# The weights stage of a graph kernel: one scalar_tensor_tensor for each tile in place of two operations for eight tiles

## What is computed

```python
def _L0_gnn_ref(x, edge_index, W, att, bias):
    h = (x @ W).reshape(N, H, C)
    row, col = (edge_index[0], edge_index[1])
    alpha = leaky_relu(s_src[row] + s_dst[col], negative_slope=0.2)
    ...
    alpha_n = ex / denom[row]
    msg = alpha_n[:, :, None] * h[col]
    out = jax.ops.segment_sum(msg, col, num_segments=N)
    return out.reshape(N, H * C) + bias
```

## Time and profile before

| | |
|---|---|
| median of three runs | 6992.02 us |
| span of the profiled execution, first to last instruction | 5519.0 us |
| difference of the two | 1473.02 us |
| PE busy (share of the span) | 4135.2 us (75%) |
| DVE busy | 3665.8 us (66%) |
| ACT busy | 3051.7 us (55%) |
| POOL busy | 3822.1 us (69%) |
| mean granted clock of PE | 0.901 |

### The profile page before, as it was taken

The page is one execution under the profiler, slowest core; times in us unless marked ns, Lnnn a source line. Parts: engine busy times, 40 slices in busy tenths (PEclk is TensorE's granted clock), DMA queues, the critical chain, the costliest instruction groups (busy, mean ns, idle before and its releaser), DMA issues. The chain is left out here.

```text
span 5519.0 us, 98800 instructions
## 1 busy us (share of the span) xinstructions
PE 4135.2 (75%) x22700; PEld 3433.9 (62%) x22897; DVE 3665.8 (66%) x7986; ACT 3051.7 (55%) x4595; POOL 3822.1 (69%) x3494
## 2 busy tenths in 40 slices
PE   4777777777777777600799977887888877887877
PEld 4666666666666666500799965666666666666665
DVE  7865444444444444439999997777777777777774
ACT  4455555545454555401677746666666666666663
POOL 2347777777777777740599955777777777777773
PEclk9988888888888888755899989999999999999998
DMA  8765555555555555494100035555555555555557
GB/s 306 262 199 148 141 139 141 139 139 139 141 139 142 138 142 140 144 68 12 57 0 0 0 78 139 145 147 146 146 144 146 146 146 146 144 146 147 146 141 104
DMA packets 1199545, 722.20 MB, mean 131 GB/s; under 512 B 929434, under 2 KB 1018452, under 8 KB 1199388
## 3 DMA queue, kind: packets, MB, share of 16 engines
q1 hardware_dynamic: 843788, 332.57, 29.7%
q0 software_dynamic: 131616, 276.04, 17.4%
q10 hardware_dynamic: 224112, 113.25, 7.2%
HBM read 559.64 MB, written 161.88 MB: 131 GB/s over the span
## 5 line engine op out<-in xcount | busy, mean ns | idle before, releaser
L1030 POOL DMA_INDIRECT g_q<-q_d,g_aux x1664 | 1574.5, 946 | 640.1 <-issue 472.4
L562 POOL DMA_INDIRECT rec_d<-rec,place x1568 | 1528.2, 975 | 499.0 <-issue 475.9
L1328 PE MATMUL g_hp<-pw,g_mix 128*128 x3328 | 883.3, 388 | 270.9 <-ACT g_mix L1224 253.4
L673 PE MATMUL lk<-tab_sd,low 128*128 128x196 f32 x3136 | 1063.1, 427 | 0.0
L1339 PE MATMUL g_ap<-g_hid,g_oh 128*128 128x256 f32 x3328 | 898.7, 393 | 165.7 <-DVE agg L1122 149.9
L611 DVE TENSOR_REDUCE rank<-equal 128x4 f32<-128x512 bf16 x392 | 262.0, 684 | 1019.1 <-ACT equal L539 1008.5
L1244 ACT ACTIVATE g_hid<-g_q 128x512 f32<-128x512 f32 x832 | 524.0, 630 | 744.8 <-DVE g_q L1108 716.2
L1108 DVE TENSOR_TENSOR g_q<-g_hp,g_q 128x512 f32<-128x512 f32 x832 | 574.8, 691 | 506.0 <-DMA g_q<-q_d,g_aux 440.6
L1328 PEld LDWEIGHTS g_hp<-pw,g_mix 128*128 128x128 f32 x3328 | 620.5, 191 | 430.3 <-issue 353.1
L1339 PEld LDWEIGHTS g_ap<-g_hid,g_oh 128*128 128x128 f32 x3328 | 587.0, 191 | 364.7 <-issue 275.1
L670 PE MATMUL lk<-mask,hx 122*128 122x245 bf16 x1568 | 483.8, 309 | 429.7 <-ACT low L528 429.7
(11 more groups left out here) (233 smaller groups left out, 5557.7 us busy)
## 6 DMA issues: line engine op xcount, KB each, us to landing
low_row<-rows_d SPq DMA_DIRECT2D x392, 256.0 KB
g_ea<-rec_d SPq DMA_DIRECT2D x208, 256.0 KB, 4.2
rec<-in_ea ACTq DMA_DIRECT2D x196, 256.0 KB
rec_d<-pad ACTq DMA_DIRECT2D x49, 936.0 KB, 3.8
hx_row<-rows_d SPq DMA_DIRECT2D x392, 98.0 KB
g_lrow<-low_row_d SPq DMA_DIRECT2D x208, 128.0 KB
g_q<-q_d,g_aux POOLq DMA_INDIRECT x1664, 2.8
rec_d<-rec,place POOLq DMA_INDIRECT x1568
```

Of the source, the lines that this page charges most:

```text
L562: pool.indirect_dma_start(rec_d, bass.IndirectOffsetOnAxis(ap=place[0:n, at, j:j + 1], axis=0), rec[0:n, at, j, :], None).then_inc(s_sc[at ...
L673: mm = pe.matmul(to[:, NB:LK], low[:, par, 1, slots], tab_sd[:, :, :].rearrange("p h a -> p (h a)"), start=False, stop=True, skip_group_ch ...
L1030: pool.indirect_dma_start(qg[:, par, j, :], None, q_d, bass.IndirectOffsetOnAxis(ap=aux[:, par, j, F_IDX - F_LOW:REC - F_LOW].bitcast(I32) ...
L1328: mm = pe.matmul(hp[u][:, k * HID:(k + 1) * HID], mix[:, par, 2 * u + k, :], pw[:, bass.ds(b[k], 1), :].rearrange("p o f -> p (o f)"), sta ...
```

## The change

For each of the eight tiles of a group, one scalar_tensor_tensor compares 0 to 48, read again for each of the four heads, with the tile's column of `high_dst`, and multiplies the result by the tile's weights. It writes the tile's 128x196 part of `oh_w` directly. The buffer `oh_high` and the semaphore `d_hi` go, with the wait on it. L1044, which writes the low one-hots of four tiles, is now the first operation of the group; the last of the eight new ones signals `d_w`. Nothing else is changed.

```diff
-            oh_high = carve(pw_flat, (2 * HEADS + 2) * S + 4 * GE, 4 * G * NB).rearrange("p (k j a) -> p k j a", k=4, j=G)
...
-            d_hi, d_w, d_acc = sem("e_high_ready"), sem("e_weights_ready"), sem("e_multiplied")
+            d_w, d_acc = sem("e_weights_ready"), sem("e_multiplied")
...
                 def weigh(g, at):
-                    tile = lambda a: a[:, bass.ds(g * G, G)]
                     if not first(g, 4):
                         v.wait_ge(d_acc, g - 3)
-                    v.tensor_tensor(oh_high[:, at, :, :], col(tile(high_dst), P, G, NB), row(iota[:, 0:NB], P, G, NB),
-                                    ALU.is_equal).then_inc(d_hi, 1)
                     v.tensor_tensor(oh_low[:, at, 0:HG, :], col(low_dst[:, bass.ds(g * G, HG)], P, HG, P),
                                     row(iota[:, :], P, HG, P), ALU.is_equal)
-                    v.wait_ge(d_hi, g + 1)
-                    v.tensor_tensor(oh_w[:, at, :, :, :], oh_high[:, at, :, :].unsqueeze(2).to_broadcast([P, G, HEADS, NB]),
-                                    al[:, :, bass.ds(g * G, G)].rearrange("p h j -> p j h")
-                                    .unsqueeze(3).to_broadcast([P, G, HEADS, NB]), ALU.mult).then_inc(d_w, 1)
+                    for j in range(G):
+                        ins = v.scalar_tensor_tensor(out=oh_w[:, at, j, :, :], in0=row(iota[:, 0:NB], P, HEADS, NB),
+                                                     scalar=high_dst[:, bass.ds(g * G + j, 1)],
+                                                     in1=al[:, :, bass.ds(g * G + j, 1)].to_broadcast([P, HEADS, NB]),
+                                                     op0=ALU.is_equal, op1=ALU.mult)
+                    ins.then_inc(d_w, 1)
```

## The result

The changed kernel takes 7094.42 us (median of four runs, 7084.29 to 7101.67), the kernel before 6989.86 us beside it (6976.08 to 7004.82). The ratio is 1.0141, with a 95% interval of 1.0125 to 1.0157: 105 us slower, where 104 were forecast (7096 against 6992).

The account below looks back on a forecast made before the run. DVE was taken to bound the weights stage, PE 0.16 us a group behind. A group grows from 2.78 to 3.28 us; 208 x 0.50 = 104 us on 6992 gives 7096 us, range 7085 to 7280.

Parts of the forecast that it names:

- The floor: Weights stage: PE's 16 loads take 2.62 us a group, so a faster DVE could win only 0.16 us a group.
- The step of one STT: Weights stage, DVE: each new 128x196 STT takes 0.333 to 0.341 us from start to start, taken as 0.335.
- three witnesses: Trace rows for the STT's fixed cost: STT at 128x1664 (0.133 us), at 128x128 (0.137), four tensor_scalar (0.195 each).
- Register work at nothing: DVE's sequencer: two addresses per STT, at most 2 x 0.075 us, covered by the 0.335 us instruction before; cost nothing.
- slips into the gaps: Weights stage: POOL's four adds might delay DVE by at most 16 us and spare 8 afterwards, 8 us net.
- PE's clock: Weights stage: the clock should hold although PE idles 0.66 us of 3.28, as in the gather stage at 1.00.
- What lies outside the span: 1473 us between the profiled span of 5519.0 and the median of 6992.02, placed outside the trace and carried over unchanged.
- The vanishing of the scalar's cost: Rival 1, weights stage: an STT takes 0.274 us, a group 2.79, time 6994 us or down to 6959; chance 0.10.
- contention on every STT: Rival 2, weights stage: POOL's contention adds 0.10 us to each STT, 270 us in all, 7262 us; chance 0.12.
- a sequencer that binds: Rival 3, DVE in the weights stage: register work adds 0.15 us to each STT, 354 us, 7346 us; chance 0.08.
- half rate: Rival 4, weights stage: STT runs at half rate, 0.538 us each, 441 us in all, 7433 us; chance 0.03.
- the lower clock: Rival 5: PE's clock falls from 2.4 to 1.2 GHz for the whole weights stage, up to 512 us, 7504; chance 0.01.

Follow-up runs that it names:

- experiment 6: The kernel before with the low one-hot of one tile in each group moved from DVE to ACT (three and five): 6970.09 us against 6996.89, ratio 0.9972.
- experiment 2: The kernel before with its multiplication cut into eight tensor_tensor of 128x196 and the compare kept: 7106.2 us.
- experiment 3: The changed kernel with the constant 3.0 as scalar instead of the column of high digits: 6999.41 us.
- experiment 5: The changed kernel with four STT of 392 elements a group instead of eight of 196, the second tile's digit and weights left out: 6994.26 us.
- experiment 1: The kernel before, unchanged, profiled once more: 7010.09 us, with a span of 7008.3 us where the first profile had 5519.0.

## Why the prediction was right

- **The bound.** DVE sets the pace, PE follows: it held before and after. The floor was read a little low: PE's loads without a wait took 2.66 us a group in experiment 6, not the 2.62 of the earlier trace rows, so that 0.12 us a group could be won and not 0.16.
- **The step of one STT.** Forecast 0.333 to 0.341, taken as 0.335, measured 0.334. One of the three witnesses does not say what the prediction has it say: the tensor_scalar of the earlier trace rows takes 0.195 us for 128 elements, which at 1.04 ns an element leaves 0.06 and not 0.13. It would show the scalar's cost only if its elements were cheaper, and no run tests that. The other two witnesses carry the estimate. The two parts of it were read from other shapes and are each measured now: 0.07 us for any instruction (experiment 2), 0.06 more for a scalar from memory (experiment 3), 1.04 ns for an element (experiment 5). The sum of the experiments closes: splitting adds 0.48 us to a group (3.26 against 2.78), eight scalars from memory add 0.48 (3.27 against 2.79), and dropping the compare, with its step of 0.47 to 0.48, takes that away once. The edit pays twice and saves once.
- **Register work at nothing.** Right; 0.093 us an instruction lies inside a step of 0.334, and the groups without it are no faster.
- **POOL.** Costed at nothing, with "slips into the gaps" as an aside of at most 16 us against 8 spared. The aside is what happened: 11 us against 8.0, net 3. As the groups cost 102 us and not 104, this also brought the total nearer to the forecast than its terms were, which is luck. The ground on which the cost was set at nothing, that POOL starves as before, was wrong; the first trace could not show it, since no STT with a scalar from memory ran beside a POOL add there.
- **PE's clock.** It stayed at 1.00 in the stage with PE idle for a fifth of it, as forecast. The ground was weaker than it looked: the gather stage's 755 of 940 us at a clock of 1.00 are those of the quick execution, and in the changed kernel's profile that stage shows 654 of 940 us at 0.85.
- **What lies outside the span.** Wrong. The prediction put 1473 us outside the trace; only some 2 us lie there (7094.12 us for the profiled execution, its span 7092.3), and the rest was in the scatter and gather stages, which ran quicker in the first profile (experiment 1). The forecast survived because the term was carried as a constant and the edit touches a stage that took the same time in both executions (experiment 1), which the prediction had not asked: that was luck. Had the change been in the gather stage, the paces and waits read from that trace would have been those of another execution. The check was at hand: a profile whose span is 21% shorter than the runs shows something else than they do, and the safe reading is to ask which stage could stretch.
- **The rivals.** The vanishing of the scalar's cost, contention on every STT, a sequencer that binds, half rate and the lower clock each had their mark in the trace, and none showed it: steps of 0.334 in the loop and out of it, ahead of POOL's adds and after them.

## What to carry to other kernels

Merging two operations into one saves only if the pass that falls away is worth more than the fixed costs that come with the new instructions. Here two instructions became eight, each paid 0.07 us to exist and 0.06 for a scalar from memory, and these 8 x 0.13 = 1.04 us outweighed the compare's step of 0.47 and the 0.07 that the one multiplication had paid; with four instructions (experiment 5) the two sides were about even. Read the fixed part from the starts of instructions back to back, not from durations, since the overlap hides it in a duration. And compare a profile's span with the timed runs before a time that lies between them is put anywhere.

## What the runs showed that was not expected

POOL's float32 adds got nothing while DVE ran tensor_tensor instructions, or STT with a constant, back to back. The first add took 557.8 us in the first profile, and all four took 669.8 us beside eight short instructions (experiment 2), where an add that is let in takes 2.4 to 4.1 us. With a scalar from memory on the STT, POOL is let in within 2 us (the first long STT starts 0.14 us after the add in the changed kernel, and 1.75 in experiment 5), one add for one STT, which then lasts 2.5 to 3.6 us in the changed kernel and 2.7 to 3.8 us in experiment 5 (four of each). The Trainium skill's page "SBUF — State Buffer", section "SBUF: two separate sides", calls the ports that the two share an exclusive lock, which the loser waits for in full. The lengths here agree with that, with STT of 3.57 us beside adds of 3.54. That the scalar's 0.06 us is the gap in which the lock changes hands is argued from experiments 2, 3 and 5, and not shown by a row.
